# First group of a two-layer graph network: the probabilities of layer 0 are turned round on TensorE instead of by DMA

## The chip, the cores and the metric

One Trainium2 chip (trn2), one core of it. The metric is the device time of one execution in microseconds, as the median of several runs. Engines: TensorE (PE, its weight loads PEld), VectorE (DVE), ScalarE (ACT), GpSimd (POOL) and SyncE (SP, which issues all DMAs here). TensorE's clock has two levels here, 1.2 and 2.4 GHz; the profile gives the granted clock as a share of the upper one.

## The reference

The input is x of 128 graphs by 64 nodes by 768 features, and an adjacency of 128 x 64 x 64. Two residual layers, each on `h = relu(layernorm(x))`:

```python
# layer 0: attention with 6 heads of 128, masked by the adjacency
q, k, v = heads(h @ Wq + bq), heads(h @ Wk + bk), heads(h @ Wv + bv)
probs = softmax(q @ k.T / sqrt(128) + where(adj, 0, -9e15))
x = x + (probs @ v) @ Wf + bf
# layer 1: 12 heads of 64, additive attention, ELU, gate
hh = h @ W; th = tanh(hh)
attn = softmax(mask(leaky_relu(th @ w_src + (th @ w_dst).T)))
o = elu(attn @ hh + b)
gate = sigmoid(h @ H_w.T + H_b)
x = x + gate * o + (1 - gate) * h
```

## The kernel before

The rows are worked through in 32 groups. A group is four graphs: T = 2 tiles of 128 partitions, two graphs of 64 nodes in each tile (called g = 0 and 1). Layer 0 of group i, layer 1 of group i - 1 and the output of group i - 2 run beside each other in one step, `one(i, now, mid, last, nxt)`, written for each engine by hand; the order of the calls in it is the order of the work on that engine. Steps 0 and 1 and the last three are written out (`first`, `second`, `tail`, `final`), the others are one hardware loop. Semaphores alone order the engines against each other.

Every product of float32 matrices is made of halves: an operand is scaled and split into a float16 high half (made by ACT) and a float16 low half (what is left, made by VectorE), and TensorE adds three products, high x high, high x low and low x high. So a row projection (`project_rows`, matmul on L581) of one tile is 18 matmuls of 512 columns and 18 of 256 (two pieces, since a PSUM bank has 512 columns), a column projection (`project_columns`, L595) takes 256 columns each. The weights are split like this once, in step 0 and 1, by ACT (`high_weight`, L1402) and VectorE (`low_weight`, L880), among the work of the first groups.

Layer 0 of step 0, by engine:

- TensorE: projections of q and k; `scores()` (L686: 24 products in float32, 64 columns each, one for each head, tile and graph, into `pair_att`); `project_v(0)`, `project_v(1)` into `pair_prj`; `context(0)`, `context(1)` (L699: for each tile 6 heads x 3 products of halves x 2 graphs); `bias_of_values()` (L621: bv times Wf, in step 0 alone, 36 matmuls as in a row projection); `project_output(0)`, `project_output(1)`.
- VectorE: `scaled_scores()` (L1056), `shift0()` (the maximum L1066, the difference L1068), `normal0()` (the sum L1073, L1075, and L1077, which gives `p0_ready`), `low_values(0)` (L1047), `p0_low()` (L1082), `low_weight(WF, 0)` and `(WF, 1)` (L880), `low_values(1)` (L1047), `split_bias_of_values()` (L863 to L874, which gives `bv_split`), `variance` (L892 to L905), `context_low` (L1103), `offset`, `fold_bias` (L1165, waits for L621), the low parts of the next group's rows (L922).
- ACT: a fill with zeros of the gaps of `e0` (L1582), the exponentials of `p0` (L1585), `high_values(0)` (L1480), the high half of the probabilities (L1591), `high_values(1)` (L1480), `context_high` (L1501), the next group's rows (L1406).
- SP: `transpose_blocks` (L482), four DMA transposes for `pt0`.

The context needs the probabilities turned round (keys on the partitions). `p0` is float32, 128 partitions (query nodes of two graphs) by 12 blocks (tile and head) of 64 keys. Before, ACT and VectorE split it into float16 halves in `e0`, where 64 columns of zeros stand between the blocks, and two DMA transposes for each half (one for each graph) bring it to `pt0`:

```python
def transpose_blocks(pt, e, landed):
    for g in range(2):
        r = slice(N * g, N * g + N)
        sp.dma_start_transpose(pt[:, :, r], e[r, (1 - g) * N:(1 - g) * N + 2 * C]).then_inc(landed, DMA)
```

`context(t)` waits for `v_ready` of its tile and for all four transposes (`pt0_landed`). `bias_of_values` comes behind both contexts in TensorE's order and waits for `bv_split`, `v_ready` and the low half of Wf. The PSUM tile `pair_att[0]` is free between VectorE's reading of the scores and `context(0)`.

Of the kernel before, what the change touches and what calls it, by code (L numbers as in the profile page):

```python
# [29 lines left out]
ALU = mybir.AluOpType  # L30
ACT = mybir.ActivationFunctionType
# [5 lines left out]
T = 2  # L37
# [44 lines left out]
def build_two_layer_gnn(nc, x, adj, wq, bq, wk, bk, wv, bv, wf, bf, wl, b1, w_src, w_dst, wg, bg, out):  # L82
# [13 lines left out]
    with ExitStack() as ctx:  # L96
# [3 lines left out]
        def sem(name):  # L100
            return ctx.enter_context(nc.semaphore(name))
# [252 lines left out]
        pt0_landed = sem("pt0_landed")  # L354
        p1_hi_made = sem("p1_hi_made")
# [84 lines left out]
        def _(sp):  # L440
# [43 lines left out]
            def one(i, now, mid, last, nxt):  # L484
# [69 lines left out]
                if now:  # L554
                    after_held(sp, transposes_held, p0_gaps, i + 1)
                    after_held(sp, transposes_held, p0_hi_made, i + 1)
                    transpose_blocks(pt0[0], e0[0], pt0_landed)
                    after_held(sp, transposes_held, p0_lo_made, i + 1)
                    transpose_blocks(pt0[1], e0[1], pt0_landed)
# [12 lines left out]
        def _(pe):  # L572
# [3 lines left out]
            def project_rows(m, lhs, t, pair, done, between=None):  # L576

                for lo, hi in ((0, 512), (512, C)) if between is None else ((512, C), (0, 512)):
                    for k in range(KT):
                        for n, (a, b) in enumerate(((0, 0), (0, 1), (1, 0))):  # L580
                            mm = nc.tensor.matmul(pair[:, lo:hi], lhs(a, k), weight(m, k, b)[:, lo:hi],  # L581
                                                  start=(k == 0 and n == 0), stop=(k == KT - 1 and n == 2))
                    if lo and between is not None:
                        between()
                mm.then_inc(done, 1)
# [52 lines left out]
            def one(i, now, mid, last, nxt):  # L638
# [23 lines left out]
                def project_v(t):  # L662
                    if first:
# [3 lines left out]
                                 pair_prj[t], v_psum)  # L667
# [22 lines left out]
                def context(t):  # L690
                    pe.wait_ge(v_ready, 2 * i + t + 1)
                    pe.wait_ge(pt0_landed, 2 * GRAPHS * (i + 1))
# [11 lines left out]
                def project_gate(t, between=None):  # L704
                    if first_mid:
# [3 lines left out]
                                 pair_prj[t], g_psum, between)  # L709
# [81 lines left out]
                if first:  # L791
                    scores()
                    project_v(0)
                    project_v(1)
# [26 lines left out]
        def _(dve):  # L821
# [208 lines left out]
            def one(i, now, mid, last, nxt):  # L1030
# [48 lines left out]

                def p0_low():  # L1080
                    dve.wait_ge(p0_hi_made, i + 1)
# [86 lines left out]
                if first:  # L1168
# [19 lines left out]
                    p0_low()  # L1188
# [204 lines left out]
        def _(act):  # L1393
# [80 lines left out]
            def one(i, now, mid, last, nxt):  # L1474
# [104 lines left out]
                if now:  # L1579
# [6 lines left out]
                    if first:  # L1586
                        high_values(0)
                    else:
                        high_values(1)
                    act.wait_ge(p0_ready, i + 1)  # L1590
                    nc.scalar.activation(blocks(e0[0]), p0, ACT.Copy, scale=P_TOP).then_inc(p0_hi_made, 1)  # L1591
                    if first:
                        high_values(1)
# [211 lines left out]
```

## Time and profile before

| what | us |
|---|---|
| median of 3 runs (lowest to highest) | 2530.87 (2529.88 to 2532.04) |
| the profiled execution, its own time | 2531.18 |
| its span, first to last instruction | 2529.4 |
| PE busy in the span | 2468.7 (98%) |
| DVE busy | 2006.6 (79%) |
| ACT busy | 912.5 (36%) |
| POOL busy | 804.1 (32%) |
| mean granted TensorE clock | 0.99 |

Times in the trace count from the first instruction; what lies outside the span (1.8 us) is the start and the end of the program. A row of a timeline merges like instructions that follow each other: start, length, engine, line, operation, what is written and read, how many, and in brackets the idle time before it and what ended it. In the chain of waits each piece released the next one, or stood before it on the same engine. Lines are those of the kernel before. A matmul of float32 shows as two records where it isn't a transpose.

### The profile page before, as it was taken

To read this page: it belongs to the slowest core of one execution; us is meant where nothing else is said; L and a number is where in the kernel's file an instruction comes from. 1 tells how busy PE (TensorE), PEld (TensorE's weight loads), DVE (VectorE), ACT (ScalarE), POOL (GpSimd) and SP (SyncE) were. 2 spreads that over 40 slices of the span, in tenths; PEclk is the share of its full clock that TensorE was granted. 3 is DMA by queue.
4 is the path that set the end of the run, shared out by engine and by line. 5 is a ranking of instruction groups with operands and counts; after the bars stand their busy time and mean duration, and the time that the engine had idled before them with its cause. 6 is when DMAs were issued, how large, how long until landed. Compare 5 with 4: busy or idle time off the path is not lost.

```text
span 2529.4 us, 54257 instructions
## 1 busy us (share of the span) xinstructions
PE 2468.7 (98%) x22592; PEld 1756.7 (69%) x22592; DVE 2006.6 (79%) x2768; ACT 912.5 (36%) x1118; POOL 804.1 (32%) x564
## 2 busy tenths in 40 slices
PE   6999999999999999999999999999999999999994
PEld 5676677776677776677776777766777766777762
DVE  7778878778778778777778777788787788787778
ACT  5434333334333233333333333333333343333332
POOL 1133332233332333332333332333323333323334
PEclk9999999999999999999999999999999999999997
DMA  9244344343343443343443343443443433443432
GB/s 303 48 90 76 76 92 86 77 87 75 78 96 80 76 94 69 81 100 75 81 82 78 84 96 71 88 79 76 89 90 73 94 72 77 94 84 75 79 62 52
DMA packets 552303, 216.98 MB, mean 86 GB/s; under 512 B 517840, under 2 KB 527056, under 8 KB 552272
## 3 DMA queue, kind: packets, MB, share of 16 engines
q1 hardware_dynamic: 552272, 216.53, 41.0%
q8 instruction: 23, 0.38, 0.1%
q14 instruction: 8, 0.07, 0.0%
HBM read 67.02 MB, written 25.17 MB: 36 GB/s over the span
## 4 chain that ended last, share of the span: by engine, by line
PE 95%; DVE 3%; DMA 1%; ACT 0%; issue 0%; POOL 0%; SPq 0%; DVEq 0%
PE pair_prj L581 58%; PE pair_prj L595 29%; PE pair_att L611 3%; PE pair_att L686 2%; PE pair_att L699 1%; PE pair_att L735 1%; DVE w_lo L880 0%; DMA arena<-in_L_gnn_Wq 0%; PE pair_prj L621 0%; PE pair_prj L722 0%; DVE w_top L840 0%; DVE w_hi L969 0%; SPq L482 0%; DMA arena<-arena 0%; DVE p_place L1159 0%
## 5 line engine op out<-in xcount | busy, mean ns | idle before, releaser
L581 PE MATMUL pair_prj<-w_hi,arena 128*128 128x512 f16 (+1 forms) x6144 | 1444.9, 326 | 3.7 <-DVE arena L1097 2.7
L581 PE MATMUL pair_prj<-w_lo,arena 128*128 128x512 f16 (+1 forms) x3072 | 1001.2, 326 | 0.0
L581 PEld LDWEIGHTS pair_prj<-w_hi,arena 128*128 128x128 f16 x6144 | 601.1, 98 | 408.2 <-DVE arena L1097 3.0
L595 PE MATMUL pair_prj<-arena,w_hi 128*128 128x256 f16 x4608 | 761.6, 273 | 3.7 <-DVE w_lo L887 3.5
L595 PE MATMUL pair_prj<-arena,w_lo 128*128 128x256 f16 x2304 | 628.9, 273 | 0.0
L595 PEld LDWEIGHTS pair_prj<-arena,w_hi 128*128 128x128 f16 x4608 | 447.3, 98 | 55.4 <-issue 3.6
L581 PEld LDWEIGHTS pair_prj<-w_lo,arena 128*128 128x128 f16 x3072 | 300.8, 98 | 194.5 <-issue 0.3
L1659 POOL TENSOR_TENSOR rstd<-var_eps,minus_half 128x2 f32<-128x2 f32 x63 | 62.8, 997 | 674.7 <-DVE var_eps L905 667.0
L595 PEld LDWEIGHTS pair_prj<-arena,w_lo 128*128 128x128 f16 x2304 | 225.8, 98 | 26.5
L1676 POOL TENSOR_TENSOR arena<-arena,b_row 128x768 f32<-128x768 f32 x60 | 108.5, 1809 | 331.1 <-DVE arena L962 331.1
L1406 ACT ACTIVATE h_hi<-arena,shift,rstd 128x768 f16<-128x768 f32 x124 | 120.6, 1019 | 212.2 <-DVE shift L910 212.2
L1711 POOL TENSOR_TENSOR arena<-arena,src_row 128x768 f32<-128x768 f32 x62 | 113.6, 1833 | 245.0 <-ACT arena L1491 241.5
L1681 POOL TENSOR_TENSOR arena<-arena 128x768 f32<-128x768 f32 x60 | 126.1, 2102 | 152.7 <-ACT arena L1437 152.7
L922 DVE TENSOR_TENSOR arena<-arena,h_hi 128x768 f16<-128x768 f32 x124 | 161.4, 1343 | 1.8 <-ACT arena L1406 1.8
L1442 ACT ACTIVATE arena<-arena 128x768 f32<-128x768 f32 x60 | 50.7, 845 | 282.8 <-DVE arena L969 282.8
L926 DVE SCALAR_TENSOR_TENSOR arena<-pair_prj,w_undo,bk_col 128x768 f32<-128x768 f32 x64 | 65.1, 1018 | 109.5 <-PE pair_prj L595 109.4
L1712 POOL TENSOR_TENSOR arena<-arena,dst_row 128x768 f32<-128x768 f32 x62 | 132.8, 2141 | 0.0
L1437 ACT ACTIVATE arena<-arena,keep_shift,keep_rstd 128x768 f32<-128x768 f32 x60 | 61.2, 1020 | 192.1 <-DVE arena L990 192.1
L1406 ACT ACTIVATE arena<-arena,shift,rstd 128x768 f32<-128x768 f32 x128 | 123.7, 1013 | 11.5 <-DVE shift L910 6.1
L892 DVE BATCH_NORM_STATS2 bn_out<-arena 128x6 f32<-128x384 f32 x252 | 121.8, 547 | 2.2 <-DMA arena<-in_x 2.2
L1507 ACT ACTIVATE arena<-arena 128x768 f32<-128x768 f32 x62 | 52.3, 844 | 184.2 <-DVE arena L1116 184.2
L1771 POOL TENSOR_TENSOR arena<-arena,bf_row 128x768 f32<-128x768 f32 x64 | 115.6, 1828 | 5.3 <-DVE bf_row L1165 5.3
(180 smaller groups left out, 2852.5 us busy)
## 6 DMA issues: line engine op xcount, KB each, us to landing
arena<-in_x SPq DMA_DIRECT2D x64, 768.0 KB, 4.4
out<-arena SPq DMA_DIRECT2D x64, 384.0 KB, 2.3
arena<-arena SPq DMA_TRANSPOSE x380, 3.4
arena<-in_L_gnn_Wq SPq DMA_DIRECT2D x2, 1152.0 KB, 8.4
arena<-in_L_gnn_Wk SPq DMA_DIRECT2D x2, 1152.0 KB, 11.8
w_hi<-in_L_gnn_Wv SPq DMA_DIRECT2D x2, 1152.0 KB, 13.4
w_lo<-in_L_gnn_Wf SPq DMA_DIRECT2D x2, 1152.0 KB, 14.4
arena<-in_L_gnn_W SPq DMA_DIRECT2D x2, 1152.0 KB, 13.6
```

What stands on the lines that cost most here:

```text
L581: mm = nc.tensor.matmul(pair[:, lo:hi], lhs(a, k), weight(m, k, b)[:, lo:hi], start=(k == 0 and n == 0), stop=(k == KT - 1 and n == 2))
L595: mm = nc.tensor.matmul(pair[:, c * 256:(c + 1) * 256], weight(m, k, a)[:, o:o + P], (ht0_hi, ht0_lo)[b][:, k, :], start=(k == 0 and n == ...
L611: mm = nc.tensor.matmul(pair_att[t][:, c], pt[:, a, :], hv[:, t, c], start=(n == 0), stop=(n == 2))
L892: bn = nc.vector.bn_stats(bn_out[n][:, t, c, :], src[:, t, c * (C // 2):(c + 1) * (C // 2)])
L922: nc.vector.tensor_tensor(h_lo[:, t, :], rows[:, t, :], h_hi[:, t, :], ALU.subtract)\
L926: nc.vector.scalar_tensor_tensor(dst[:, 3 * half:3 * half + 3, :], pair[:, 0:C].rearrange("p (c n) -> p c n", c=3), col(w_undo, m), bias[: ...
L1406: return nc.scalar.activation(dst[:, t, :], src[:, t, :], ACT.Relu, bias=shift[n][:, t:t + 1], scale=rstd[n][:, t:t + 1])
L1676: nc.gpsimd.tensor_tensor(o, o, b1_row[:].unsqueeze(1).broadcast_to([P, H1, E1]), ALU.add)\
L1681: nc.gpsimd.tensor_tensor(held(g)[:, t, :], held(g)[:, t, :], scratch(t, g)[2], ALU.add)\
L1711: nc.gpsimd.tensor_tensor(by_src, th, src_row[:], ALU.mult).then_inc(src_prod, 1)
L1712: nc.gpsimd.tensor_tensor(by_dst, th, dst_row[:], ALU.mult).then_inc(dst_prod, 1)
L1771: nc.gpsimd.tensor_tensor(x1[:, t, :], x1[:, t, :], bf_row[:], ALU.add).then_inc(bf_added, 1)
```

## The change

In step 0 alone, TensorE turns the probabilities: between the two pieces of `project_v(1)` it multiplies each 64 x 64 block of `p0` (as the stationary operand, float32) with the identity, into `pair_att[0]`: 12 blocks x 2 graphs, 24 products. ACT takes the high half out of PSUM straight into `pt0`, one instruction for each graph (64 partitions by 768), and VectorE the low half, also one for each graph. The four DMA transposes of this group, the fill of the gaps and the two halves in `e0` go; the context waits for `pt0_lo_made` in place of the transposes. ACT's copies stand between `high_values(0)` and `high_values(1)`; VectorE's `turned_low()` stands where `p0_low()` stood. All other steps stay as they are, with the counts of their semaphores one lower. The order of the two pieces of a projection becomes an argument, with the same values as before for every other call.

```diff
--- before.py
+++ after.py
@@ -352,6 +352,9 @@
         p0_lo_made = sem("p0_lo_made")
         p0_gaps = sem("p0_gaps")
         pt0_landed = sem("pt0_landed")
+        p0_turned = sem("p0_turned")
+        pt0_hi_made = sem("pt0_hi_made")
+        pt0_lo_made = sem("pt0_lo_made")
         p1_hi_made = sem("p1_hi_made")
         p1_lo_made = sem("p1_lo_made")
         p1_gaps = sem("p1_gaps")
@@ -551,11 +554,11 @@
                     after_alone(sp, eye_made, full_made[1], 2 * j + 2)
                     after_alone(sp, eye_made, kept, j + 1)
                     sp.dma_start(x1, x_g[i]).then_inc(x1_loaded, DMA)
-                if now:
-                    after_held(sp, transposes_held, p0_gaps, i + 1)
-                    after_held(sp, transposes_held, p0_hi_made, i + 1)
+                if now and not first:
+                    after_held(sp, transposes_held, p0_gaps, i)
+                    after_held(sp, transposes_held, p0_hi_made, i)
                     transpose_blocks(pt0[0], e0[0], pt0_landed)
-                    after_held(sp, transposes_held, p0_lo_made, i + 1)
+                    after_held(sp, transposes_held, p0_lo_made, i)
                     transpose_blocks(pt0[1], e0[1], pt0_landed)
                 if nxt:
                     after_held(sp, transposes_held, v_psum, 2 * i + 2)
@@ -573,14 +576,16 @@
             def weight(m, k, part):
                 return (w_hi, w_lo)[part][:, m, k, :]
 
-            def project_rows(m, lhs, t, pair, done, between=None):
-
-                for lo, hi in ((0, 512), (512, C)) if between is None else ((512, C), (0, 512)):
+            WIDE_FIRST, NARROW_FIRST = ((0, 512), (512, C)), ((512, C), (0, 512))
+
+            def project_rows(m, lhs, t, pair, done, between=None, pieces=WIDE_FIRST):
+
+                for lo, hi in pieces:
                     for k in range(KT):
                         for n, (a, b) in enumerate(((0, 0), (0, 1), (1, 0))):
                             mm = nc.tensor.matmul(pair[:, lo:hi], lhs(a, k), weight(m, k, b)[:, lo:hi],
                                                   start=(k == 0 and n == 0), stop=(k == KT - 1 and n == 2))
-                    if lo and between is not None:
+                    if between is not None and (lo, hi) == pieces[0]:
                         between()
                 mm.then_inc(done, 1)
 
@@ -659,12 +664,21 @@
                     project_rows(WL, lambda a, k: (ht1_hi, ht1_lo)[a][:, k, t * P:(t + 1) * P], t,
                                  pair_prj[t], h_psum)
 
-                def project_v(t):
+                def turn_probabilities():
+                    pe.wait_ge(p0_ready, 1)
+                    for a in range(T * H0):
+                        for g in range(2):
+                            r = slice(g * N, (g + 1) * N)
+                            mm = nc.tensor.matmul(pair_att[0][r, a * N:(a + 1) * N], p0[r, a, :], ident[r, r], start=True,
+                                                  stop=True)
+                    mm.then_inc(p0_turned, 1)
+
+                def project_v(t, between=None):
                     if first:
                         pe.wait_ge(weight_ready, made_ready(WV, 1))
                     pe.wait_ge(k_ready, 2 * i + t + 1)
                     project_rows(WV, lambda a, k: (ht0_hi, ht0_lo)[a][:, k, t * P:(t + 1) * P], t,
-                                 pair_prj[t], v_psum)
+                                 pair_prj[t], v_psum, between)
 
                 def attend(t):
                     if t == 0:
@@ -689,7 +703,10 @@
 
                 def context(t):
                     pe.wait_ge(v_ready, 2 * i + t + 1)
-                    pe.wait_ge(pt0_landed, 2 * GRAPHS * (i + 1))
+                    if first:
+                        pe.wait_ge(pt0_lo_made, 2)
+                    else:
+                        pe.wait_ge(pt0_landed, 2 * GRAPHS * i)
                     pt0_hi, pt0_lo = pt0
                     parts0 = ((vals_hi, pt0_hi), (vals_hi, pt0_lo), (vals_lo, pt0_hi))
                     for h in range(H0):
@@ -706,7 +723,7 @@
                         pe.wait_ge(weight_ready, made_ready(WG, 1))
                     pe.wait_ge(h_ready, 2 * j + t + 1)
                     project_rows(WG, lambda a, k: (ht1_hi, ht1_lo)[a][:, k, t * P:(t + 1) * P], t,
-                                 pair_prj[t], g_psum, between)
+                                 pair_prj[t], g_psum, between, WIDE_FIRST if between is None else NARROW_FIRST)
 
                 def logit_operands():
 
@@ -791,7 +808,7 @@
                 if first:
                     scores()
                     project_v(0)
-                    project_v(1)
+                    project_v(1, between=turn_probabilities)
                 elif now:
                     project_v(0)
                     scores()
@@ -1077,8 +1094,18 @@
                     nc.vector.tensor_tensor(p0, p0, rinv0[:].unsqueeze(2).broadcast_to(wide), ALU.mult)\
                         .then_inc(p0_ready, 1)
 
+                def turned(place, g):
+                    return place[g * N:(g + 1) * N, :, g * N:(g + 1) * N]
+
+                def turned_low():
+                    for g in range(2):
+                        dve.wait_ge(pt0_hi_made, g + 1)
+                        nc.vector.scalar_tensor_tensor(turned(pt0[1], g), heads1(pair_att[0][g * N:(g + 1) * N, 0:C]),
+                                                       P_TOP, turned(pt0[0], g), ALU.mult, ALU.subtract)\
+                            .then_inc(pt0_lo_made, 1)
+
                 def p0_low():
-                    dve.wait_ge(p0_hi_made, i + 1)
+                    dve.wait_ge(p0_hi_made, i)
                     nc.vector.scalar_tensor_tensor(blocks(e0[1]), p0, P_TOP, blocks(e0[0]), ALU.mult, ALU.subtract)\
                         .then_inc(p0_lo_made, 1)
 
@@ -1185,7 +1212,7 @@
                     shift0()
                     normal0()
                     low_values(0)
-                    p0_low()
+                    turned_low()
                     low_weight(WF, 0)
                     low_weight(WF, 1)
                     low_values(1)
@@ -1576,21 +1603,27 @@
 
                 if nxt and not first and not second:
                     normalise_next()
-                if now:
+                if first:
+                    act.wait_ge(shifted0, 1)
+                    nc.scalar.activation(p0, p0, ACT.Exp).then_inc(exp0_ready, 1)
+                    high_values(0)
+                    act.wait_ge(p0_turned, 1)
+                    for g in range(2):
+                        r = slice(g * N, (g + 1) * N)
+                        nc.scalar.activation(pt0[0][r, :, r],
+                                             pair_att[0][r, 0:C].rearrange("p (a n) -> p a n", n=N), ACT.Copy, scale=P_TOP)\
+                            .then_inc(pt0_hi_made, 1)
+                    high_values(1)
+                elif now:
 
                     act.wait_ge(s_psum, 2 * i + 2)
                     nc.scalar.activation(gaps(19 * C), zero[:].unsqueeze(2).unsqueeze(3).broadcast_to([P, 2, GAPS, N]),
                                          ACT.Copy).then_inc(p0_gaps, 1)
                     act.wait_ge(shifted0, i + 1)
                     nc.scalar.activation(p0, p0, ACT.Exp).then_inc(exp0_ready, 1)
-                    if first:
-                        high_values(0)
-                    else:
-                        high_values(1)
+                    high_values(1)
                     act.wait_ge(p0_ready, i + 1)
                     nc.scalar.activation(blocks(e0[0]), p0, ACT.Copy, scale=P_TOP).then_inc(p0_hi_made, 1)
-                    if first:
-                        high_values(1)
                 if second:
                     act.wait_ge(weight_ready, made_ready(WG, 1))
                 if mid:
```

## Rows read from the trace of the kernel before

**Rows 1.** The page, part 4: the chain that ended last, by engine.
```profile
PE 95%; DVE 3%; DMA 1%; ACT 0%; issue 0%; POOL 0%; SPq 0%; DVEq 0%
```

**Rows 2.** The list of TensorE's waits: for whom, total us, times, longest.
```profile
PE pair_att L699 <- DMA arena<-arena: 4.3, 1, 4.3
```

**Rows 3.** TensorE's timeline: start us, us, engine, line, what, count [idle before].
```profile
59.52 0.27 PE L581 MATMUL pair_prj<-w_lo,arena 128*128 128x256 f16 x1
...
61.26 0.27 PE L581 MATMUL pair_prj<-w_hi,arena 128*128 128x256 f16 x1
65.88 2.10 PE L699 MATMUL pair_att<-arena,p_place 64*128 64x64 f16 x72 [4.34 <-DMA arena<-arena]
68.47 0.61 PE L621 MATMUL pair_prj<-w_hi,p_place 128*128 128x512 f16 x1 [0.49 <-DVE p_place L874]
```

**Rows 4.** The chain of waits from 0 to 130 us: start us, us, what.
```profile
56.56 0.96 DVE p_place L1047
...
58.39 5.06 DVE w_lo L880 x2
...
67.39 1.03 DVE p_place L874
...
68.47 7.24 PE pair_prj L621 x36
...
110.99 5.85 PE pair_prj L581 x36
```

**Rows 5.** SP's timeline, 44 to 80 us; DMA queues, 57 to 66 us.
```profile
57.35 6.36 SPq L482 DMA_TRANSPOSE arena<-arena  x4
...
DMA packets 3201, 0.80 MB, mean 89 GB/s; under 512 B 3200, under 2 KB 3200, under 8 KB 3200
```

**Rows 6.** ACT's timeline, first group.
```profile
52.81 0.84 ACT L1585 ACTIVATE p_place<-p_place 128x768 f32<-128x768 f32 x1 [1.01 <-DVE p_place L1068]
55.72 0.81 ACT L1480 ACTIVATE p_place<-pair_prj 128x768 f16<-128x768 f32 x1 [2.07 <-PE pair_prj L581]
56.43 0.83 ACT L1591 ACTIVATE arena<-p_place 128x768 f16<-128x768 f32 x1
```

**Rows 7.** VectorE's timeline, first group.
```profile
54.94 0.96 DVE L1077 TENSOR_TENSOR p_place<-p_place,rinv 128x768 f32<-128x768 f32 x1
...
57.44 0.95 DVE L1082 SCALAR_TENSOR_TENSOR arena<-p_place,arena 128x768 f16<-128x768 f32 x1
58.31 5.14 DVE L880 SCALAR_TENSOR_TENSOR w_lo<-w_lo,w_scale,w_hi 128x2304 f16<-128x2304 f32 x2
```

**Rows 8.** Nearest operations: TensorE's timeline, then VectorE's groups by shape (mean ns).
```profile
116.77 1.62 PE L686 MATMUL pair_att<-arena 128*64 128x64 f32 x48
118.32 0.39 PE L581 MATMUL pair_prj<-w_hi,arena 128*128 128x512 f16 x1
...
2456.14 0.87 PE L648 MATMUL pair_att<-ident,arena 128*128 128x128 f32 x6
...
9.84 2.79 PE L602 MATMUL pair_prj<-ident,arena 128*128 128x128 f32 x12 [9.84 <-ACT arena L1406]
...
L1047 DVE SCALAR_TENSOR_TENSOR p_place<-pair_prj,p_place 128x768 f16<-128x768 f32 x64 | 60.9, 952 | 4.1 <-ACT p_place L1480 4.1
L1139 DVE TENSOR_TENSOR arena<-pair_prj,of_head 108x768 bf16<-108x768 f32 x64 | 60.6, 949 | 0.5 <-PE pair_prj L718 0.5
```

**Rows 9.** Windows: us, busy us and count of PE, PEld, DVE, ACT, POOL, granted clock, DMA share, GB/s.
```profile
68.50:71.00 2.50, 2.50 (x7) 0.86 (x8) 2.43 (x8) 0.39 (x2) 0.06 (x1) 0.51 0.00 0
71.00:75.70 4.70, 4.70 (x32) 3.03 (x31) 1.70 (x5) 2.96 (x4) 0.68 (x1) 1.00 0.01 3
...
19.00:23.00 4.00, 3.92 (x19) 2.84 (x20) 4.00 (x3) 4.00 (x5) 0.00 (x0) 0.50 1.06 374
23.00:24.00 1.00, 1.00 (x10) 0.86 (x9) 1.00 (x2) 1.00 (x2) 0.60 (x1) 0.91 1.06 372
```

**Rows 10.** TensorE's timeline, its first wait behind L621.
```profile
2460.30 2.10 PE L611 MATMUL pair_att<-arena 128*128 128x64 f16 x36 [3.28 <-DVE arena L1230]
```

## The prediction

> **What bounds the kernel now.** I read the page first. PE is busy 98% of the span and holds 95% of the chain that ended last [rows 1]: thirty-two groups follow each other at TensorE's pace, and what delays TensorE in the first group comes out at the end unless a later wait swallows it. So I looked for TensorE's waits. One of the longest is what the change is about: the context products of layer 0 (L699) waited 4.3 us for the DMA that brings the turned probabilities [rows 2]. TensorE's timeline puts it in place, and shows another of 0.5 us before L621, ended by L874: V ends at 61.53 (61.26 + 0.27), the 72 context products run from 65.88 to 67.98, the bias products of L621 start at 68.47 [rows 3].
>
> From this alone the 4.3 us look like a prize. The chain of waits, cut to this stretch, says otherwise [rows 4]. It does not go through the DMA at all. It holds ACT's L1480, then an unbroken run of VectorE: L1047, L1082 (the low half of the probabilities), two L880 (the low half of Wf, 5.06 us), L1047, the scales, L872, L874, and only then TensorE's L621. The context floats: had it started at 61.6 it would have ended 4 us earlier, and `bias_of_values` would still have waited for `bv_split` until 68.42. **In this stretch VectorE is the bound**, so the question is what the change does to VectorE's order.
>
> **Part 1, removed: four DMA transposes, VectorE's L1082, ACT's L1591 and its gap fill L1582 (first group only).** The transposes are issued from 57.35 on and the context starts at 65.88 [rows 3, 5]; off the path, worth nothing directly. SP issues them for 6.36 us. The next thing on its queue are the transposes of group 1's rows, which wait for ACT's rows made behind the context, so an earlier SP moves nothing, and POOL's queue is not touched. Nor does another load gain: between 57 and 66 us the DMA engines carry 0.80 MB in 3201 packets, all but one under 512 B, which are the transposes' own, and no load of a weight [rows 5]. The gap fill ran while ACT had nothing else: ACT still idled 1.01 us before Exp (L1585), which waits for VectorE's L1068 [rows 6]; without the fill it idles longer. L1591 ran beside VectorE's L1047. L1082 gives VectorE back 0.87 us from start to start (57.44 to 58.31) [rows 7].
>
> Here a rule is to be weighed. The row has four transposes in 6.36 us of issue alone, 1.6 each [rows 5]. The Trainium skill (VectorE: DVE Perf Modes, The three transpose paths) gives 390 ns for a 128 by 128 block turned by TensorE against 1309 ns by the DMA's crossbar, and advises TensorE where PSUM will do as the target. By that rule the change would be a gain; of its two figures the trace bears on the DMA's alone, and shows it no faster. The rule prices the operation and says nothing of who waits for it. What a gain would be here, from rows, is rival (b).
>
> **Part 2, added on TensorE: 24 f32 products of 64 columns between V's two pieces.** Their wait, `p0_ready`, is given by L1077, which ends at 55.90 [rows 7]: over when the wide piece is. The narrow piece of V (t = 1) starts at 59.52 [rows 3]; the turning takes that place and everything behind it on TensorE moves by its length. The nearest row are the scores, L686: also 24 f32 products in code, 64 moving columns, 48 records, 1.55 us until the next instruction starts (116.77 to 118.32) [rows 8]. A second row agrees: six f32 turns of 128 columns (L648) take 0.87 us with the last one's 0.27 in it, so 0.12 each, 0.06 for 64 columns, 1.44 for 24 [rows 8]. I take 1.55. Lower bound 0.8: one record in place of two. Upper bound 2.8: the same f32 turns at the kernel's start (L602) took 2.79 us for twelve, 0.23 for 128 columns [rows 8]. With the drain the turning is done at 59.52 + 1.62 = 61.14, and V at 63.1. TensorE pays nothing for it: it was idle from 61.5 to 65.9.
>
> **Part 3, added on ACT: two copies out of PSUM, 64 partitions by 768.** The wait for `p0_turned` has `high_values(1)` queued behind it, then the context's high halves. The first copy starts at 61.18. The nearest row is L1480, 128 partitions by 768 from PSUM: 0.81 us, and 0.71 to the start of the next [rows 6]. I take it whole for 64 partitions. They end at 61.99 and 62.70.
>
> **Part 4, on VectorE: `turned_low` in `p0_low`'s place.** This is what costs. VectorE is through L1047 at 57.44 and now stands before `pt0_hi_made` until 62.02, 4.6 us of idle it did not have. Then two instructions instead of one, 0.87 each from start to start: 62.02 and 62.89. An instruction on 108 partitions (L1139) has a mean of 949 ns, one on 128 (L1047) 952 [rows 8], so fewer partitions look no cheaper; the bound below is 0.87 saved, above nothing. `low_weight(WF, 0)` starts at 63.76 instead of 58.31: **+5.45 us**. Queued behind it are both L880, `low_values(1)`, the scales, L872, L874, all in the chain [rows 4]. `low_values(1)` needs ACT's high half of V, there by 63.9 against 68.8: covered. So L621 starts at 68.47 + 5.45 = 73.92.
>
> **Part 5, TensorE's clock.** Before, it is granted half (0.51 of full, 1.2 of 2.4 GHz) in L621's first 2.5 us, 68.50 to 71.00, and full behind that [rows 9]: 1.25 us lost, which agrees with L621's 7.24 us beside 5.85 for 36 like products of L581 [rows 4]. After the change TensorE has context(0) at 63.9, idles 4.8 us until `v_ready` lets context(1) go at 69.8, and idles 3.1 us more before L621. The nearest row for dense products behind such gaps is the kernel's beginning: from 19.08 the clock was 0.50 for four us, and 0.91 in the fifth [rows 9]. So 4.1 us at half, 2.05 lost: **+0.8**. Lower bound 0, as before; less is excluded by the two gaps, since one of 4.3 us was enough to bring it down. Upper bound: six us at half, +1.75.
>
> **Behind it.** `fold_bias`, the low parts of group 1's rows and their transposes hang on L621 and shift with it. From L621 on, TensorE's next wait is at 2460.30 [rows 10], in the last groups, and ended by VectorE, which shifts alike: nothing swallows the delay. The later groups' code is the same, with counts one lower.
>
> **Sum.** 5.45 + 0.8 = 6.25 us. The profiled execution took 2531.18 us (span 2529.4 and 1.8 around it), so 2537.4; it stands 0.3 above the median of the three runs, 2530.87. For the median: **2537.1 us**, 0.25% more.
>
> **Rivals.** (a) *Same mechanism, too small to measure.* Within 0.2% (5.1 us) is about what a measurement of this kernel can't tell from no change. Turning in 0.8 takes 0.75 off, cheaper 64-partition work 0.87, a clock back as early as before 0.8. Two of the three give +4.6 to +4.7, 2535.5; all three +3.8, 2534.7; one alone still leaves +5.4. For it: none of the three is seen in the trace of before. Against it: 108 partitions cost what 128 do, and L648 agrees with L686. 20%.
>
> (b) *Faster.* The wait for the DMA was the bound and is gone: TensorE goes from V through context to L621 without a pause and its clock never falls, so 4.3 and 1.25 us come back, 2525.3 us. The Trainium skill's rule on the three paths points this way. The place is `bias_of_values`' wait for `bv_split`; it decides for a gain only if VectorE gives `bv_split` before 68.42, and all of the run that leads there is in the chain, with 4.6 us of new idle ahead of it [rows 4]. 3%.
>
> (c) *Slower still.* Turning in 2.8 us (+1.25), six us at half clock (+0.95), or both: 2538.1 to 2539.3. For it: f32 turns were that slow once, at the start. Against: the clock is full at 59, as it was at 116. 12%.
>
> The forecast has 65%. It and (c) are slower by over 0.2%: 77%; within: 20%; faster: 3%. The range goes from (a) with all three, 2534.7, to (c) with both, 2539.3, and 0.3 more on either side, since the runs shown lie 2.2 us apart: 2534.4 to 2539.6.
>
> **What the changed profile would show.** 48 new f32 records, 1.6 us from 59.5. VectorE idle for 4.6 us before the first low half, ended by ACT; two low halves of 0.95; the first L880 of Wf at 63.8. TensorE: 0.8 idle before the first context, 4.8 between the two, 3.1 before L621, ended by L874 at 73.9; L621 near 8.0 us. If L621 still starts before 70, VectorE was not held and the mechanism is wrong; if it starts at 74 and the total is under 2535.9, something later swallowed part of it.

## The result and the profile after

| | us |
|---|---|
| before, median of 14 runs (lowest to highest) | 2531.53 (2529.88 to 2533.06) |
| after, median of 14 runs | 2537.53 (2536.60 to 2538.68) |
| ratio of the two, 95% interval | 1.0024 (1.0017 to 1.0031) |
| profiled execution after, its own time; span | 2536.66; 2534.9 |

The change costs 6.0 us, 0.24%. The distance arises in the first group, between 57 and 82 us. One run of the kernel before among those beside e1 to e4 took 9194.88 us and is left out of all that follows. Lines of the changed kernel are some higher than before: turning L672, ACT's high half L1613, VectorE's low half L1103, context L716, bias products L626 (before L621), Wf L897 (before L880).

The chain of waits of the changed kernel, 50 to 84 us (start us, us, what):

```profile
59.41 1.57 PE pair_att L672 x48
...
61.00 0.81 ACT arena L1613
...
61.84 0.95 DVE arena L1103
...
62.82 0.96 DVE arena L1103
...
63.81 5.15 DVE w_lo L897 x2
...
68.99 0.96 DVE p_place L1064
...
73.03 1.03 DVE p_place L891
...
74.10 7.66 PE pair_prj L626 x36
```

Against [rows 4] the run of VectorE from the low halves of Wf to L626 is the same work. What is new stands ahead of it: turning, ACT, two low halves, where there was one low half that waited for nothing. Wf starts at 63.81, before at 58.31. VectorE's timeline (start us, us, engine, line, what, idle before) has the hole:

```profile
56.41 0.96 DVE L1064 SCALAR_TENSOR_TENSOR p_place<-pair_prj,p_place 128x768 f16<-128x768 f32 x1 [0.68 <-ACT p_place L1507]
61.84 1.94 DVE L1103 SCALAR_TENSOR_TENSOR arena<-pair_att,arena 64x768 f16<-64x768 f32 x2 [4.47 <-ACT arena L1613]
```

VectorE is through the low half of V at 57.37 and waits 4.47 us for ACT, which waits for TensorE. TensorE's own timeline:

```profile
59.34 1.61 PE L672 MATMUL pair_att<-ident,p_place 64*64 64x64 f32 x48
...
63.93 0.70 PE L716 MATMUL pair_att<-arena,p_place 64*128 64x64 f16 x36 [0.90 <-DVE arena L1103]
70.01 1.14 PE L716 MATMUL pair_att<-arena,p_place 64*128 64x64 f16 x36 [5.38 <-DVE p_place L1064]
74.10 0.61 PE L626 MATMUL pair_prj<-w_hi,p_place 128*128 128x512 f16 x1 [2.96 <-DVE p_place L891]
```

The wait for the DMA of 4.34 us [rows 3] is gone, and three take its place: 0.90 before the first context, 5.38 between the contexts, 2.96 before L626. Together they are 4.4 us longer than the two waits that they replace (4.34 and 0.49). The granted clock (windows: us, busy us and counts, then the clock, DMA share and GB/s as the last three):

```profile
76.00:77.00 1.00, 1.00 (x3) 0.30 (x2) 0.96 (x5) 0.00 (x0) 0.43 (x1) 0.50 0.00 0
77.00:78.00 1.00, 1.00 (x5) 0.44 (x4) 1.00 (x3) 0.00 (x0) 0.30 (x1) 0.78 0.00 0
78.00:79.00 1.00, 1.00 (x7) 0.41 (x6) 0.33 (x2) 0.63 (x1) 0.00 (x0) 1.00 0.00 0
```

It is at half until about 77.4, so for the first 3.3 us of L626, which takes 7.66 us against 7.24 before [rows 4, 9].

The two traces, in one sum: both count from the first instruction, and the changed one runs 0.16 us ahead when the scores start (46.97 against 47.13). L626 ends 6.05 us later than L621 did (81.76 against 75.71). The spans are 5.5 apart; the rest was given back in the last groups, where TensorE's waits came out 0.3 to 0.4 shorter for some and longer for one, for instance the wait that was 2.75 before. Part of it is clock, and no edit reaches there: the 36 products behind TensorE's wait at 2460 (L611, here L616) took 2.10 us before [rows 10], at a granted clock of 0.50, then 1.80 in the change at 0.61, and 1.22 in e4 (below) at 1.00.

```profile
2466.37 1.80 PE L616 MATMUL pair_att<-arena 128*128 128x64 f16 x36 [3.27 <-DVE arena L1257]
...
2485.05 0.39 PE L586 MATMUL pair_prj<-w_hi,arena 128*128 128x512 f16 x1 [2.39 <-DVE arena L1124]
```

```profile
2465.62 1.22 PE L611 MATMUL pair_att<-arena 128*128 128x64 f16 x36 [3.27 <-DVE arena L1231]
```

In every trace of this record TensorE's next V starts 16.8 to 17.0 us behind the end of these 36, so the time of a run holds up to 0.9 us that has nothing to do with the first group.

### The profile page after: what moved, and what is told of

It is laid out like the page before. It is cut to its first block, busy times and chain, and to the rows that moved or that the text cites. A ratio compares the mean times of both kernels' runs of the same rounds, so it can differ in the third digit from the quotient of the medians.

```text
span 2534.9 us, 54349 instructions
## 1 busy us (share of the span) xinstructions
PE 2470.9 (97%) x22640; PEld 1757.5 (69%) x22640; DVE 2007.2 (79%) x2769; ACT 913.2 (36%) x1118; POOL 804.0 (32%) x564
## 4 chain that ended last, share of the span: by engine, by line
PE 95%; DVE 3%; DMA 1%; ACT 0%; issue 0%; POOL 0%; SPq 0%; DVEq 0%
PE pair_prj L586 58%; PE pair_prj L600 29%; PE pair_att L616 3%; PE pair_att L700 2%; PE pair_att L716 1%; PE pair_att L752 1%; DVE w_lo L897 0%; DMA arena<-in_L_gnn_Wq 0%; PE pair_prj L626 0%; PE pair_prj L739 0%; DVE w_top L857 0%; DVE w_hi L986 0%; SPq L485 0%; DMA arena<-arena 0%; DVE p_place L1186 0%
```

## The experiments

Theory: VectorE bounds this stretch. Its idle time before `turned_low` and the second low half pass undiminished to the bias products, and TensorE's clock adds its part. Rivals: the wait for the DMA was the bound; TensorE's added products or the reading of PSUM are what costs; the clock is no cause.

All differences below are against the runs of the kernel before on the same chip, as medians of 11 runs or more. An interval of a ratio is 0.0009 wide to either side, some 2.3 us, in every experiment: which of two neighbours is faster is often not settled by it alone. The ratio on record is not the ratio of the two medians; for e3 it stands for 1.0 us where the medians are 1.84 apart. So the traces are read beside both. "Start" is the distance from the start of the instruction that gives `p0_ready` (L1077 before) to the start of the bias products, less that of before (68.47 - 54.94 = 13.53); "length" is that of the bias products.

| run | start | length | time - before | ratio (95%) |
|---|---|---|---|---|
| before | 0 | 7.24 | 0 | |
| the change | +5.80 | 7.66 | +6.00 | 1.0024 (1.0017 to 1.0031) |
| e1 turned_low behind Wf | +1.10 | 8.26 | +1.08 | 1.0005 (0.9995 to 1.0014) |
| e2 VectorE without idle time | +0.65 | 8.47 | +1.42 | 1.0004 (0.9995 to 1.0013) |
| e3 before + turning | +1.47 | 8.57 | +1.84 | 1.0004 (0.9995 to 1.0013) |
| e4 before + wait | +4.14 | 8.55 | +4.23 | 1.0017 (1.0008 to 1.0026) |
| e5 e2 kept busy | +1.38 | 6.02 | -1.55 | 0.9995 (0.9986 to 1.0004) |
| e6 change kept busy | +5.80 | 6.02 | +3.31 | 1.0014 (1.0005 to 1.0023) |
| e7 before kept busy | 0.00 | 6.02 | -1.57 | 0.9994 (0.9985 to 1.0003) |
| e8 turned ahead of V | +2.25 | 7.47 | +1.92 | 1.0009 (1.0000 to 1.0018) |
| e9 e7, largest of bv early | -1.06 | 6.02 | -3.01 | 0.9989 (0.9980 to 0.9998) |
| e10 e3 kept busy | +1.34 | 6.02 | -1.44 | 0.9996 (0.9987 to 1.0005) |
| e11 e4 kept busy | +4.15 | 6.02 | +2.64 | 1.0010 (1.0001 to 1.0019) |
| e12 e5, turned ahead of V | +1.45 | 6.02 | +0.02 | 0.9999 (0.9990 to 1.0008) |

Two things keep "start" and "length" from adding up to the time. From the end of the bias products to the end of the span it took 2453.7 us in the trace of before, the longest of the fourteen, and 2452.2 in those of e2, e3 and e4, the shortest; part of it are the 36 products named above. And in the profiled executions of e3, e5, e10 and e12 the clock had fallen around the scores. V's first tile came later by it, and some 0.7 us of their "start" are this and no edit: VectorE waited 1.3 to 1.4 us for the high half of V (t = 0), against 0.6 to 0.7 in the others. Counted from the start of VectorE's low half of V (t = 0) instead, which is behind that wait, the bias products of these four start 0.70 to 0.73 us later than before, and those of e2 0.71. VectorE's row of before:

```profile
56.56 0.96 DVE L1047 SCALAR_TENSOR_TENSOR p_place<-pair_prj,p_place 128x768 f16<-128x768 f32 x1 [0.67 <-ACT p_place L1480]
```

"Kept busy" means products of 512 columns that fill TensorE's waits and whose result nothing reads:

```python
def busy(n):
    for m in range(n):
        nc.tensor.matmul(pair_prj[0][:, 0:512], weight(WQ, m % KT, 0)[:, 0:P], weight(WV, m % KT, 0)[:, 0:512],
                         start=True, stop=True)
```

### e1: the low halves of Wf go first

```diff
                     low_values(0)
-                    turned_low()
                     low_weight(WF, 0)
                     low_weight(WF, 1)
+                    turned_low()
                     low_values(1)
```

> Edit: the changed kernel, with VectorE's turned_low moved behind both low halves of Wf. Theory (VectorE's idle time before turned_low is the cost): VectorE goes from the low half of V straight into Wf at 57.3, is through at 62.3, finds the high halves long there, and has 1 us more than before to do (two low halves of 0.98 instead of one of 0.87). The bias products start near 69.4 instead of 74.1; they last 5.9 to 7.3 us, by the clock. Total 4.7 to 6.1 us below the changed kernel, so -0.4 to +1.1 us against the kernel before. Rival (the cost lies in TensorE's products or in reading PSUM at 64 partitions): the bias products still start at 74 and the total stays 5 to 6 us above before.

VectorE's timeline, then TensorE's, of e1:

```profile
57.31 5.13 DVE L897 SCALAR_TENSOR_TENSOR w_lo<-w_lo,w_scale,w_hi 128x2304 f16<-128x2304 f32 x2
62.37 1.93 DVE L1103 SCALAR_TENSOR_TENSOR arena<-pair_att,arena 64x768 f16<-64x768 f32 x2
```

```profile
69.44 0.61 PE L626 MATMUL pair_prj<-w_hi,p_place 128*128 128x512 f16 x1 [3.39 <-DVE p_place L891]
```

No idle time: Wf from 57.31, the low halves at once when their turn comes, bias products at 69.44 as expected. 2532.10 us, +1.08: 4.9 of the 6.0 us are gone, and TensorE still turns and PSUM is still read by halves. The rival that puts the cost there falls; what is left for it is about the 1.1 us by which the start is later, and the second low half (0.98) is most of that.

### e2: no idle time, and the bias scales early

```diff
                     shift0()
+                    largest_bias()
                     normal0()
                     low_values(0)
+                    scale_bias_of_values()
+                    low_weight(WF, 0)
                     turned_low()
-                    low_weight(WF, 0)
-                    low_weight(WF, 1)
                     low_values(1)
+                    low_weight(WF, 1)
                     split_bias_of_values()
```

`largest_bias` is the reduction over bv (L880 of the changed kernel, 0.94 us), `scale_bias_of_values` the eight small scales, and `split_bias_of_values` keeps the two halves.

> Edit: the changed kernel with another order on VectorE: the largest of bv in the wait for Exp, its scales behind the low half of V (t = 0), then the first half of Wf, turned_low, low half of V (t = 1), second half of Wf, and the two halves of bv last. Theory: of the 12.1 us that VectorE has to do from 57.3 on 0.95 go into a wait that was idle anyway, some 0.5 of idle time before turned_low may be left; bias products start near 68.9. Total 5.2 to 6.6 us below the changed kernel, -0.9 to +0.6 against before. Both contexts follow each other near 64 to 66, so the clock may stay full: then at the lower end. Rival (cost in TensorE's products or in PSUM reads): no better than +5 against before.

TensorE's chain in e2, and its clock:

```profile
68.91 8.47 PE pair_prj L626 x36
```

```profile
72.00:73.00 1.00, 1.00 (x4) 0.32 (x3) 1.00 (x4) 0.00 (x0) 0.12 (x1) 0.50 0.00 0
73.00:74.00 1.00, 1.00 (x4) 0.34 (x3) 0.14 (x2) 0.82 (x1) 0.00 (x0) 0.55 0.00 0
74.00:75.00 1.00, 1.00 (x6) 0.45 (x5) 0.00 (x0) 1.00 (x2) 0.00 (x0) 1.00 0.00 0
```

The start came as expected (68.91), the gain didn't: +1.42. The products took 8.47 us, since the clock stayed at half for their first 5.0 us. I had thought that it might hold through the gap of 3.4 us; it fell in the gap, at about 67, and the products met it near its beginning and not near its end. What starts earlier can meet more of the half clock. The total is 0.8 us above the range that I had given; the interval of its ratio reaches from 0.9995 to 1.0013, so it doesn't show a loss either.

### e3 and e4: turning alone, and waiting alone

e3 adds `turn_probabilities` between V's pieces as the change has it, with the transposes still there and its result unread. Its edit also has a wait of VectorE for `p0_turned` ahead of `split_bias_of_values`, which was over 3 us before VectorE came there (62.54 against 66.37). e4 adds one line:

```diff
                     low_values(0)
+                    dve.wait_ge(v_psum, 2)
                     p0_low()
```

> Edit: the kernel before, with the 24 turning products added between V's pieces and their result not used; the four DMA transposes stay. Theory: TensorE was idle from 61.5 to 65.9, so 1.55 us more of products cost nothing: 0.0 us, or down to -1.4 if the shorter idle time keeps the clock full. Rival (turning is exposed): +1.5 us.

> Edit: the kernel before, with one wait added: VectorE's low half of the first group's probabilities waits until V (t = 1) is done, near 61.6, instead of starting at 57.4. Nothing is turned on TensorE. Theory: 4.2 us of idle time on VectorE push the bias products from 68.5 to 72.7, and the clock gives up to 0.8 more: +4.2 to +5.0 us. The late DMA transposes bring the context to about 69, still ahead of the bias products. Rival (VectorE has slack there): +1 or less. Rival (the context's wait for DMA is what counts): +3, as late as the transposes come.

VectorE's timeline of e4, then the chain's last step:

```profile
61.46 0.96 DVE L1082 SCALAR_TENSOR_TENSOR arena<-p_place,arena 128x768 f16<-128x768 f32 x1 [4.05 <-PE pair_prj L581]
```

```profile
72.50 8.55 PE pair_prj L621 x36
```

One wait of 4.05 us on VectorE and nothing else moves the start by 4.14 us, though the DMA had long delivered when the bias products start (the context ran from 67.28). This is the core of the change's cost without the change. That the total is +4.23, inside what was expected, is partly luck: the length adds 1.31 in the trace, more than the 0.8 allowed for, and 1.4 are given back behind the bias products.

e3 missed: +1.84, not 0. TensorE's timeline and VectorE's show two reasons, and the length of the bias products (8.57) a third:

```profile
47.80 2.29 PE L696 MATMUL pair_att<-arena 128*64 128x64 f32 x48 [1.94 <-DVE arena L936]
```

```profile
57.99 0.96 DVE L1057 SCALAR_TENSOR_TENSOR p_place<-pair_prj,p_place 128x768 f16<-128x768 f32 x1 [1.43 <-ACT p_place L1491]
...
65.50 0.96 DVE L1057 SCALAR_TENSOR_TENSOR p_place<-pair_prj,p_place 128x768 f16<-128x768 f32 x1 [0.62 <-ACT p_place L1491]
```

The 1.6 us of turning move V's second tile, and VectorE, which used to find its high half waiting, idles 0.62 for ACT; the start moves by 0.70 through this. This I had not seen: before, that high half was there 0.98 us ahead of VectorE (62.38 against 63.36), less than the turning takes:

```profile
61.57 0.81 ACT L1480 ACTIVATE p_place<-pair_prj 128x768 f16<-128x768 f32 x1 [4.31 <-PE pair_prj L581]
```

```profile
63.36 0.95 DVE L1047 SCALAR_TENSOR_TENSOR p_place<-pair_prj,p_place 128x768 f16<-128x768 f32 x1
```

In the changed kernel it is covered by VectorE's own delay. The other part is clock: in this profiled execution it had fallen already around the scores (48 records in 2.29 us instead of 1.62), which moves the start by another 0.77, and again before the bias products, which adds 1.33 of length. That is no part of the edit.

### e5, e6, e7: the clock taken out

e5 is e2 with `busy(14)` ahead of the bias products; e6 the changed kernel with `busy(22)` between the contexts and `busy(12)` behind them; e7 the kernel before with `busy(18)` in the wait for the transposes.

> Edit: e2 (VectorE without idle time), and 14 products of 512 columns on TensorE, written where nothing reads them, between the second context and the bias products (3.0 us in a gap of 3.4). Theory (what e2 lost it lost to the clock, which fell at 67 and stayed at half through the first 5.0 us of the bias products): the clock stays full, the bias products take 5.9 us instead of some 8.4, the total is 2.5 us below e2, some 1 us below the kernel before. Rival (the clock's half speed is no cause, e2 is late for another reason): same as e2, or later if the added products delay the bias products.

> Edit: the changed kernel, with 22 such products between the two contexts (4.75 us in a gap of 5.4) and 12 behind them (2.6 us in 3.0). Theory: only the clock's part of the change's cost goes: the bias products still start at 74.1 but take 5.9 us instead of 7.7, total 1.7 us lower in the profile, 4.3 us above the kernel before instead of 6.0. VectorE's stall remains as 5.6 us. Rival (the added products make it dearer or nothing changes): 6 us or more above before.

> Edit: the kernel before, with 18 such products in TensorE's 4.3 us wait for the DMA transposes. Theory: the bias products still start at 68.5 but at full clock, 5.9 us instead of 7.2: 1.3 us below before; the wait for the DMA then cost nothing but the clock. Rival (the wait for the DMA bounds the bias products): no gain.

The bias products in the chain of e6 and of e7, and e7's context on TensorE:

```profile
73.93 6.02 PE pair_prj L626 x36
```

```profile
68.14 6.02 PE pair_prj L621 x36
```

```profile
65.89 1.22 PE L706 MATMUL pair_att<-arena,p_place 64*128 64x64 f16 x72 [0.79 <-DMA arena<-arena]
```

All three have 6.02 us for the bias products; the clock is out of them. e7 is the clearest: the context waits until 65.89 for the DMA, as before, the products start where they started (13.53 us behind `p0_ready`'s instruction in both), and they take 1.22 us less for work that nothing reads. The medians are 1.57 apart, though the interval (0.9985 to 1.0003) still includes no gain. So the wait for the DMA cost the kernel before only its clock. e5 is 3.0 us below e2 by the medians, where 2.5 was expected, and e6 3.3 above before, where 4.3 was. With the clock out of both, the change costs 3.31 + 1.57 = 4.9 us between e7 and e6 in the medians and 5.8 in the two traces' starts. So of its 6.0 us the clock's part is 1.1 by the medians and 0.42 by the lengths in the traces (7.66 - 7.24); the runs don't settle it closer.

### e8: the same order on VectorE, turned earlier

```diff
-                    project_v(1, between=turn_probabilities)
+                    turn_probabilities()
+                    project_v(1)
```

> Edit: the changed kernel, with the turning products ahead of V (t = 1) instead of between its pieces, VectorE's order as changed. Theory: the probabilities are ready at 55.7, the turning is done at 57.3, the first high half at 58.2, so VectorE idles some 0.9 us instead of 4.5 before turned_low; the bias products start 3.6 us earlier, near 70.5. Their length depends on the clock: 5.9 to 8.5 us. Total 2.8 to 4.5 us below the changed kernel, 1.5 to 3.2 above before. Rival (place in TensorE's order does not matter): as the changed kernel, 6 above before.

```profile
55.23 1.61 PE L672 MATMUL pair_att<-ident,p_place 64*64 64x64 f32 x48 [0.27 <-DVE p_place L1095]
...
69.99 0.61 PE L626 MATMUL pair_prj<-w_hi,p_place 128*128 128x512 f16 x1 [3.12 <-DVE p_place L892]
```

```profile
57.72 1.94 DVE L1104 SCALAR_TENSOR_TENSOR arena<-pair_att,arena 64x768 f16<-64x768 f32 x2 [0.93 <-ACT arena L1614]
```

TensorE waits 0.27 us for `p0_ready`, VectorE idles 0.93 instead of 4.47, and the start moves from +5.80 to +2.25. 2533.56, +1.92: within what was expected. The stall's length follows the place of the turning in TensorE's order.

### e9: faster than both

e7, and the reduction over bv in VectorE's wait for Exp:

```diff
                     shift0()
+                    largest_bias()
                     normal0()
```

> Edit: e7 (the kernel before, TensorE kept busy in its wait for the DMA), and VectorE takes the largest of bv (0.95 us) into its idle wait for Exp. Theory (VectorE's run up to the two halves of bv bounds the bias products, not the DMA): bias products start 0.9 us earlier, near 67.2, just behind the context, at full clock: 0.9 us below e7, some 2.5 below before. Rival (the wait for the DMA bounds them): same as e7.

```profile
66.09 1.22 PE L706 MATMUL pair_att<-arena,p_place 64*128 64x64 f16 x72 [0.66 <-DMA arena<-arena]
67.49 0.39 PE L621 MATMUL pair_prj<-w_hi,p_place 128*128 128x512 f16 x1 [0.18 <-DVE p_place L883]
```

The products start 1.06 us earlier than before and 0.18 us behind the context: only here is the DMA's wait close to being the bound. Without it little would be won, since VectorE gives `bv_split` at 67.44 (66.42 + 1.02), just ahead of them. 2528.56 us, 3.0 below before, the only version here whose interval lies wholly below 1.

### e10, e11: e3 and e4 with the clock full

e10 is e3 with `busy(12)` ahead of the context and `busy(6)` behind it; e11 is e4 with `busy(25)` and `busy(16)`.

> Edit: e3 (the kernel before with the turning products added, unused) with 12 filling products of 512 columns in what is left of the wait for the DMA and 6 between context and bias products, so that the clock stays full. Theory (turning costs TensorE nothing, and e3 was 1.4 to 1.8 above before by the clock alone, which came back only after 5.2 us of its bias products): same as e7 within 0.3 us, 1.4 to 1.7 below before. Rival (turning itself costs): above e7 by 1.4 or more.

> Edit: e4 (the kernel before with VectorE's low half of the probabilities held until V is done) with 25 filling products ahead of the context and 16 behind it. Theory: with the clock full the stall stands alone: VectorE's 4.05 us, so 4.05 above e7 (2.4 to 2.7 above before). Rival (some of VectorE's stall is taken up elsewhere): 3 us or less above e7.

e10's VectorE, then e11's VectorE and its first bias product:

```profile
65.14 0.96 DVE L1065 SCALAR_TENSOR_TENSOR p_place<-pair_prj,p_place 128x768 f16<-128x768 f32 x1 [0.62 <-ACT p_place L1499]
```

```profile
61.01 0.96 DVE L1090 SCALAR_TENSOR_TENSOR arena<-p_place,arena 128x768 f16<-128x768 f32 x1 [4.05 <-PE pair_prj L581]
```

```profile
72.05 0.39 PE L621 MATMUL pair_prj<-w_hi,p_place 128*128 128x512 f16 x1
```

e10 is 0.1 us above e7 in the medians, but its trace has the same 0.62 of idle time before the low half of V as e3, and moves the start by 0.71 behind the low half of V (t = 0). So turning costs between 0.1 and 0.7, through ACT's high half of V and not through TensorE's own time; the runs can't settle it closer. e11 is 4.2 us above e7 (2.64 + 1.57) and starts its bias products 4.15 later, for 4.05 us of idle time: a stall of VectorE here comes out whole.

### e12: the change, with all that helps it

e5 with the turning ahead of V (t = 1) and `busy(12)`.

> Edit: e5 (the changed kernel, VectorE's order without idle time, TensorE kept busy behind the contexts), with the turning ahead of V (t = 1) and 12 filling products. Theory: VectorE's last 0.4 us of idle time go, the bias products start some 0.4 us earlier than in e5, at full clock; 0.4 below e5, 1.6 to 2 below before. It still has the extra low half (1.0 us) that the kernel before doesn't have, so it stays some 1 us behind e9. Rival (without the transposes the context comes sooner and gains something): level with e9 or better.

```profile
65.63 0.96 DVE L1075 SCALAR_TENSOR_TENSOR p_place<-pair_prj,p_place 128x768 f16<-128x768 f32 x1 [0.64 <-ACT p_place L1520]
```

Missed: level with before instead of 1.6 to 2 below, and not better than e5. VectorE's idle time before `turned_low` is gone, but 0.64 us stand before the low half of V now, since V's second tile is behind the turning. The two cancel, and the traces put e12 level with e5: the bias products start at +1.45 against +1.38 with the same length, and the profiled executions took 2531.46 and 2531.36 us. The 1.6 us between their distances to before, taken on two chips with overlapping intervals, are not shown to be an effect of the edit. It stays 3 us behind e9 (0.7 of it the clock around the scores, by the traces), so none of the orders tried beats the transposes when both get the same help.

## Why the prediction was right

- **VectorE is the bound; the context floats.** Right, and shown from both sides: e4 and e11 (a stall alone costs what it lasts), e7 (the products start at the same place with the DMA's wait filled), e1 (the stall goes, 4.9 us go).
- **Part 1, transposes worth nothing on the path.** Right: what they cost was clock (e7), 1.22 us in the length of the bias products.
- **Part 2, turning 1.55 us from 59.52.** 48 records, 59.34 to 60.95, the next piece of V at 60.89: 1.55 from start to start. Right. That TensorE pays nothing is right for this kernel alone; in the order of before it costs up to 0.7 through V's high half (e3, e10), which the prediction did not look at as a term of its own.
- **Part 3, full price for 64 partitions on ACT.** 0.81 for one, right; two took 1.64, without the overlap of 0.1 that was taken from L1480 (61.18 to 62.70 is 1.52). Nothing waited for the second.
- **Part 4, +5.45.** The start moved by 5.80. The idle time was 4.47. The 4.6 predicted count from 57.44, the start of L1082; L1047 ends at 57.52 [rows 4], from where the same working gives 4.50. The term mis-sized is the low half: 0.98 from start to start, not 0.87 (61.84, 62.82, then 63.81), 0.22 for the two, and 0.13 more between Wf's start and V's low half (5.18 against 5.05).
- **Part 5, the clock, +0.8.** The profile has 3.3 us at half instead of 4.1, and a length of 7.66 instead of about 8.0: +0.42. By the medians the clock's share is 1.1 (e6, e7). So the value was twice what this trace has, inside the bounds given (0 to +1.75). The row it was taken from, the kernel's beginning, did not carry over, and the same 36 products met 2.5 to 5.2 us of half clock over the runs, so the kernel before could not give the value. TensorE's waits were 0.90, 5.38 and 2.96 against 0.8, 4.8 and 3.1 predicted; context(0) ran at full clock.
- **Behind it.** Predicted was that nothing swallows the delay. No wait did so by design, but 0.5 us of the 6.05 were given back in the last groups, 0.3 of it by the clock there.
- **Sum.** 5.80 + 0.42 = 6.2 in the trace, 6.0 in the medians, 6.25 predicted. The mechanism is right; that the sum is this close is luck, since start was 0.35 too low and clock 0.38 too high. The forecast of 2537.1 stood on a median before of 2530.87, which came out as 2531.53 with more runs. Rivals (b) and (c) did not come: no gain, no turning of 2.8 us. Rival (a)'s three savings did not show either, except for the smaller share of the clock.
- **The rule of the three transpose paths** (the Trainium skill, VectorE: DVE Perf Modes) is not contradicted as to the whole operation: 24 products of 64 by 64 took 1.6 us on TensorE, the four transposes 6.36 us of issue alone. The prediction's reading of the row was wrong, though: it set 1.6 us of issue beside the page's figure for one 128 by 128 block, but each of these transposes turns 64 by 1536 elements, six times as much. That is an estimate of 0.27 us of issue for each block's worth, and 0.36 from the first issue to the context's start (8.53 us for 24). The price did not decide. Before, the transposes were not on the path. In the changed kernel the turning is (in e8 it comes 3.55 us earlier behind `p0_ready`, and the bias products start 3.55 earlier), and what makes it so is the pick-up from PSUM, which stands in ACT's and VectorE's order.

## What to carry to other kernels

A wait of the busiest engine is worth only as much as the chain goes through it: follow the chain before removing it, and look at whose order the replacement's work enters. When a result moves from a DMA to engines, the in-order engine that picks it up must have other work ahead of the pick-up, or it stands still with all that is queued behind. A wait of TensorE that bounds nothing can still cost its clock; filling it with products that nothing reads took 1.22 us off the products behind it here (e7).

## What the runs showed of the hardware

- The half clock met by the same 36 products lasted 2.5 us (before), 3.3 (the change), 4.6 (e1), 5.0 (e2) and about 5.2 (e3, e4), lengths 7.24 to 8.57 against 6.02 when kept busy, and it does not order by the gap ahead of them: 0.49 us behind a context at half clock before, 3.4 in e2 and e1, 1.86 in e3. Executions also differ in whether it falls around the scores near 50 us (e3, e5, e10 and e12 did, the others not) and in the last groups (36 products in 1.22 us at a granted clock of 1.00 in e4, 2.10 at 0.50 before). The runs of one kernel lie 1.6 to 3.9 us apart; the last groups' part of that is 0.9, and that the clock is most of the rest is argued from these lengths, not shown.
- Float16 context products took 0.70 us for 36 at full clock (e6, granted 1.00) and 1.14 at half (the change, granted 0.50).
- An instruction on 64 partitions is as dear as on 128: ACT 0.81, VectorE 0.95. Two low halves out of PSUM followed each other with 0.03 us between them, where L1082 and its successor overlapped by 0.08; why is open.
